# The first FFN of eight items spread anew over ten calls of a macaron block's pipeline

## The chip, the cores and the metric

One core of one Trainium2 chip. The metric is the time of one launch in device microseconds, median of several runs. The engines are named as the profile names them: PE or TensorE (matmuls), DVE or VectorE, ACT or ScalarE, POOL or GpSimd, SP (which here only issues DMAs). Each takes its own instructions in the order in which they are written, and waits on semaphores.

## The reference

Eight items of 256 tokens by 256 features go through one macaron block:

```
x = x + 0.5 * ffn(layernorm(x))     # first FFN
x = x + attn(layernorm(x))          # Mamba mixer and MLP, each with its own rmsnorm and residual
x = x + 0.5 * ffn(layernorm(x))     # second FFN, the same weights
```

`ffn` is a mixture of 32 experts of 96 hidden columns, of which each token uses 6 (sigmoid scores, top 6, normalised), and a shared expert of 192. The kernel computes all experts densely and multiplies by the combine weights, which are zero where an expert isn't used: 3264 hidden columns in 26 chunks of 128. `attn` is a Mamba mixer (512 channels, 16 states, a convolution of 4 taps, a scan over the 256 tokens) and a gated MLP of 1024. Everything is float32, at float32 accuracy.

## The kernel before

**A pipeline over steps.** The outer loop runs over t = -1 to 9. In step t an item t - 1 is in its Mamba mixer, item t - 2 in its MLP, and there is one call of the FFN, whose columns are tokens. A call is narrow (256 columns, one item) or wide (512 columns, two items): `spans` holds the columns of each step. A wide call joins a slot "f1" (columns 0 to 255) and a slot "f2" (columns 256 to 511); both use each chunk's weights once, at half the weight loads per item. Before the change the calls are: step 0 item 0's first FFN, narrow; step 1 items 1 and 2 together, wide; step 2 item 3, narrow; steps 3 to 6 the first FFN of item t + 1 and the second FFN of item t - 3, wide; step 7 the second FFN of items 4 and 5, wide; steps 8 and 9 the second FFN of item 6, then 7, narrow.

**A chunk of a call.** `glu_half` (L737 to L739) makes 6 matmuls for g and 6 for u, float32 split into two parts of fp32r (`x_hi`, `x_lo` times the halves of `wr`). ScalarE takes a tanh (L980) and copies u (L970), VectorE multiplies (L1107), GpSimd multiplies by u (L1376) and by the combine weights (L1384), and four more matmuls (L818) add the down product into `acc`, three chunks later. At the call's end VectorE adds `acc` to the residual (`end`, L1133). Every third chunk has a selection matmul, `cmb`, for the combine weights.

**Step 0** also prepares the weights: each raw chunk is loaded (`raw`, 256 KB), split by ScalarE (`ws`, L949) and VectorE (L1113) into two halves, and the halves are stored to DRAM (`keep_w`, 512 KB), from where all later calls load them (`wl`, `wln`) into six slots. Step 0 has no Mamba and no MLP.

**Norms and routing.** `norm(...)` is four items: mean by a matmul (`n1`), subtraction (`nc`, L1165), variance by a matmul (`n2`), multiply (`nm`, L1176). `routing` is a matmul and eight short pieces on VectorE (`rt1`, `rq`); `rt2` transposes the result into `comb`, `hx` splits the normed x into `x_hi` and `x_lo`. `ln1` and `ln1b` prepare a first FFN, `ln2` and `ln2a` a second.

**Mamba.** `front(0, ...)` and `front(1, ...)` are the projections, convolution and softplus of each half of the channels. Then there are 32 units: in each, two selections by matmul, a multiply, a scan (L1271) and a multiply on VectorE, and a sum on GpSimd. The first front half of an item is either made in the step before ("next", beside the units of the previous item) or, where x1, the result of the first FFN, isn't there in time, in the item's own step before its first unit ("own"). Before the change steps 1 and 2 have an own front half; steps 2 to 7 have a next one.

**The order** of all engines comes from one list per step, `items_of(t)`. `merge(heavy, light, WEIGHT)` lays the light items (Mamba, norms, routing) evenly beside the heavy ones (MLP and FFN) by hand-set lengths; the last `TAIL` = 6 items of the FFN come after all light ones. An own front is at the head of the light list.

**x1 and its residuals.** The first FFN adds into `x1` or into `x1_next`, which is loaded with the item's x beforehand (`again`, `again_n`); `shift` copies `x1_next` to `x1` by a DMA once `r0` has read the old one. `x2kept` holds the residual of the second FFN in slot "f2" (`keep` copies it, `store` writes the output).

Of the kernel before, what the change touches and what calls it, by code (L numbers as in the profile page):

```python
# [33 lines left out]
P = 128  # L34
SEQ, BATCH, DM = 256, 8, 256
# [32 lines left out]
    "again_n": {"x_again_n": 16},  # L68
    "shift": {"shifted": 16},
# [51 lines left out]
STARTS = {"x2_free": 16}  # L121
# [30 lines left out]
def routing(call):  # L152
    return [("rt1", call)] + [("rq", call, i) for i in range(len(ROUTE))]
# [59 lines left out]

def items_of(t):


    if t < 0:
        return [("load", 0)] + norm("ln1") + routing("f1")
# [104 lines left out]
def ffn_items(t):  # L323
# [6 lines left out]
    for p in range(FFN_CHUNKS + DLAG):  # L330
        now, before = p < FFN_CHUNKS, 1 <= p <= FFN_CHUNKS
        out += [("cmb", "ff", p // 3)] if p < ROUTED and p % 3 == 0 else []
# [102 lines left out]
def macaron_kernel(nc, d):  # L435
# [8 lines left out]
    spans = [(0, 2 * SEQ if t == 1 or 3 <= t < BATCH else SEQ) for t in times]  # L444
# [3 lines left out]
    with ctx:  # L448
# [29 lines left out]
        x1_next = sb("x1_next", [P, KC, SEQ])  # L478
# [38 lines left out]
        parts = sb("parts", [P, PARTS, 2, SEQ], BF16)  # L517
        rows = nc.dram_tensor("rows", [3, P, PARTS, 2, SEQ], BF16, kind="Internal").ap()
# [105 lines left out]
        def _(sp):  # L624
# [6 lines left out]
            def do(s, it):  # L631
                if it[0] == "load":
# [5 lines left out]
                    item = s.t() + (1 if times[s.n] < 0 or it == ("load", 0) and times[s.n] == 0 else 2)  # L638
                    sp.dma_start(xin[:], d["x"][item]).then_inc(sem["x_loaded"], 16)
                    if s.n == 0:  # L640
# [63 lines left out]
                if it[0] == "shift":  # L704
# [15 lines left out]
            sp.wait_ge(sem["x2_free"], STARTS["x2_free"] + 16 * BATCH)  # L720
# [3 lines left out]
        def _(pe):  # L724
# [18 lines left out]
            def do(s, it):  # L743
# [77 lines left out]
                elif kind_of(it) == "n1c":  # L821
# [4 lines left out]
                    elif it[1] == "lnA":  # L826
                        pe.wait_ge(sem["shifted"], s.count("shifted", ("shift",), 16))
# [18 lines left out]
                elif kind == "rt1":  # L846
                    if s.n == 0:
                        pe.wait_ge(w_small, 16 * 4)
                    norm = next(n for n in NORMS_OF[it[1]] if ("nm", n) in s.at)
                    pe.wait_ge(sem["normed"], s.count("normed", ("nm", norm), 1))  # L850
# [9 lines left out]
                elif kind == "rt2":  # L860
# [6 lines left out]
                    for tt in range(TT):  # L867
# [615 lines left out]
```

## Time and profile before

| | |
|---|---|
| time, median of 3 runs | 1793.62 us (1792.89 to 1794.39) |
| the profiled execution | 1797.3 us, span 1795.5 us |
| mean granted TensorE clock | 0.947 of full speed |
| busy PE, PE weight loads | 1556.8 us (87%), 1136.3 us (63%) |
| busy DVE, ACT, POOL | 1288.6 us (72%), 842.9 us (47%), 993.8 us (55%) |
| moved by DMA | 200.25 MB, mean 112 GB/s |

Busy shares are means over the whole span. A step is taken here as the stretch from one call's last residual addition to the next call's: the ends are at 116.2, 314.8, 528.4, 727.6, 927.3, 1125.6, 1324.6, 1537.6, 1693.8 and 1795.5 us, steps 0 (with -1) to 9. Within a step, "scan 0", "scan 16" and "scan 31" are the starts of the first, the 17th and the last scan of its 32 units. Matmuls are pipelined, so their bars overlap and a busy TensorE need not be at its peak.

### The profile page before, as it was taken

To read this page: it belongs to the slowest core of one execution; us is meant where nothing else is said; L and a number is where in the kernel's file an instruction comes from. 1 tells how busy PE (TensorE), PEld (TensorE's weight loads), DVE (VectorE), ACT (ScalarE), POOL (GpSimd) and SP (SyncE) were. 2 spreads that over 40 slices of the span, in tenths; PEclk is the share of its full clock that TensorE was granted. 3 is DMA by queue.
4 is the path that set the end of the run, shared out by engine and by line. 5 is a ranking of instruction groups with operands and counts; after the bars stand their busy time and mean duration, and the time that the engine had idled before them with its cause. 6 is when DMAs were issued, how large, how long until landed. Compare 5 with 4: busy or idle time off the path is not lost. (4 is left out here: it accounts for less than half of the span.)

```text
span 1795.5 us, 22504 instructions
## 1 busy us (share of the span) xinstructions
PE 1556.8 (87%) x7088; PEld 1136.3 (63%) x7088; DVE 1288.6 (72%) x2085; ACT 842.9 (47%) x1676; POOL 993.8 (55%) x1048
## 2 busy tenths in 40 slices
PE   6878888777788999899998999899985999868979
PEld 5756555655676666666666666666663666647868
DVE  4536995478968878687959887887857776679421
ACT  4434543545624563356534663456433553445323
POOL 2523676345545766376646666476633766348525
PEclk9989999978989999999999999999996999979989
DMA  6863223332332323242333223232321332224434
GB/s 220 318 206 98 78 82 101 96 100 85 101 105 90 115 84 110 70 138 78 111 102 118 83 90 112 85 129 84 105 79 41 123 100 102 82 86 158 145 104 147
DMA packets 72278, 200.25 MB, mean 112 GB/s; under 512 B 9921, under 2 KB 22433, under 8 KB 71777
## 3 DMA queue, kind: packets, MB, share of 16 engines
q1 hardware_dynamic: 63968, 173.65, 29.1%
q0 software_dynamic: 8192, 25.17, 4.8%
q8 instruction: 57, 0.93, 0.2%
q14 instruction: 61, 0.49, 0.1%
HBM read 173.62 MB, written 23.59 MB: 110 GB/s over the span
## 5 line engine op out<-in xcount | busy, mean ns | idle before, releaser
L737 PE MATMUL gub<-x_hi,wr 128*128 128x512 f32 (+1 forms) x1040 | 425.4, 409 | 50.6 <-DVE hid L1107 44.8
L1397 POOL TENSOR_TENSOR ring<-ring 128x512 f32<-128x512 f32 x192 | 253.6, 1321 | 307.4 <-DVE ring L1277 306.2
L1376 POOL TENSOR_TENSOR hid<-hid,u_sb 128x512 f32<-128x512 f32 (+1 forms) x260 | 289.6, 1114 | 236.1 <-ACT u_sb L970 199.0
L818 PE MATMUL acc<-hid,w_down 128*128 128x512 f32 (+1 forms) x1040 | 408.9, 519 | 1.8 <-POOL hid L1376 1.8
L739 PE MATMUL gub<-x_hi,wr 128*128 128x512 f32 (+1 forms) x1040 | 370.8, 357 | 0.0
L738 PE MATMUL gub<-x_lo,wr 128*128 128x512 f32 (+1 forms) x1040 | 370.2, 356 | 0.0
L1271 DVE TENSOR_TENSOR_SCAN ring<-decays,side 128x512 f32<-128x512 f32 x256 | 310.5, 1213 | 28.9 <-ACT decays L1069 24.6
L970 ACT ACTIVATE u_sb<-gub 128x512 f32<-128x512 f32 (+1 forms) x260 | 132.7, 510 | 347.3 <-PE gub L739 346.8
L980 ACT ACTIVATE hid<-gub 128x256 f32<-128x256 f32 (+1 forms) x324 | 156.8, 484 | 278.2 <-PE gub L739 153.7
L1384 POOL TENSOR_TENSOR hid<-hid,weight 128x512 f32<-128x512 f32 (+1 forms) x240 | 272.9, 1137 | 15.8
L737 PEld LDWEIGHTS gub<-x_hi,wr 128*128 128x128 f32 x1040 | 205.4, 197 | 93.6 <-issue 58.1
L818 PEld LDWEIGHTS acc<-hid,w_down 128*128 128x128 f32 x1040 | 189.2, 197 | 97.2 <-issue 80.8
L1069 ACT ACTIVATE decays<-dts,a_neg 128x255 f32<-128x255 f32 x512 | 228.8, 497 | 3.8 <-DVE ring L1271 3.6
L1262 DVE TENSOR_TENSOR side<-dtx,side 128x512 f32<-128x512 f32 x256 | 176.8, 690 | 69.0 <-PE side L912 68.3
L739 PEld LDWEIGHTS gub<-x_hi,wr 128*128 128x128 f32 x1040 | 204.6, 197 | 27.1
L738 PEld LDWEIGHTS gub<-x_lo,wr 128*128 128x128 f32 x1040 | 205.8, 198 | 24.4 <-issue 5.5
L1107 DVE SCALAR_TENSOR_TENSOR hid<-hid,gub 128x512 f32<-128x512 f32 (+1 forms) x260 | 149.0, 573 | 98.3 <-ACT hid L980 98.3
L1277 DVE TENSOR_TENSOR ring<-ring,side 128x512 f32<-128x512 f32 x256 | 176.0, 687 | 59.5 <-PE side L915 36.2
L885 PE MATMUL side<-rn,w_in 128*128 128x256 f32 x448 | 120.4, 417 | 18.7 <-DVE ring L1271 13.5
L912 PE MATMUL side<-bst,sel_b 96*128 96x256 bf16 x512 | 103.7, 285 | 33.9 <-DVE ring L1271 18.1
L915 PE MATMUL side<-cst,sel_c 96*128 96x256 bf16 x512 | 103.9, 286 | 33.2 <-DVE ring L1271 32.7
L779 PE MATMUL gub<-xn_mlp,wm_gu 128*128 128x256 f32 x512 | 122.4, 387 | 0.0
(120 smaller groups left out, 1823.3 us busy)
## 6 DMA issues: line engine op xcount, KB each, us to landing
wr<-w_halves SPq DMA_DIRECT2D x234, 512.0 KB, 3.3
wm_gu<-in_w_mlp POOLq DMA_DIRECT2D x64, 256.0 KB, 3.1
w_halves<-wr SPq DMA_DIRECT2D x26, 512.0 KB, 4.9
wm_down<-in_w_mlp POOLq DMA_DIRECT2D x64, 128.0 KB, 2.6
w_raw<-in_w_gu SPq DMA_DIRECT2D x26, 256.0 KB, 4.3
rows<-parts SPq DMA_DIRECT2D x16, 384.0 KB, 2.3
cst<-rows SPq DMA_DIRECT2D x48, 128.0 KB, 2.6
xin<-in_x SPq DMA_DIRECT2D x8, 256.0 KB, 2.9
```

The costliest lines, as they stand in the source:

```text
L737: mm(out, w[:, 0, half, k, :], x_hi[:, k, a:b], start=(k == 0), stop=False)
L738: mm(out, w[:, 0, half, k, :], x_lo[:, k, a:b], start=False, stop=False)
L739: last = mm(out, w[:, 1, half, k, :], x_hi[:, k, a:b], start=False, stop=(k == KC - 1))
L818: last = mm(acc[k][:, a:b], w, h[:, a:b], start=(c == 0), stop=(c == (MLP_CHUNKS if mlp else FFN_CHUNKS) - 1))
L980: A(hid[c % HSLOTS][:, a:b], s.gub_of(it)[:, a:b], ACT.Tanh, scale=0.5).then_inc(sem["tanh_done"], 1)
L1069: A(decay[u % 2][:, h, 1:SEQ], dts[:, j, 1:SEQ], ACT.Exp, scale=a_neg[:, j, n:n + 1]).then_inc(sem["decay"], 1)
L1262: v.tensor_tensor(b, twice(dtx[:, j, :]), b, ALU.mult).then_inc(sem["driven"], 1)
L1271: v.tensor_tensor_scan(w.rearrange("p h s -> p (h s)"), decay[u % 2][:, :, :].rearrange("p h s -> p (h s)"), s.side_of(("ub", u))[:, :], 0 ...
L1277: v.tensor_tensor(w, w, pair(s.side_of(it)), ALU.mult).then_inc(sem["read_out"], 1)
L1376: nc.gpsimd.tensor_tensor(h, h, u_sb[c % USLOTS][:, a:b], ALU.mult).then_inc(sem["hidden"], 1)
L1384: nc.gpsimd.tensor_tensor(h, h, weight[c // 3 % CSLOTS][:, a:b], ALU.mult).then_inc(sem["weighted"], 1)
L1397: add(ysum, ysum, ring[:, u % 3], ALU.add).then_inc(sem["y_sum"], 1)
```

## The change

The first FFN runs earlier: items 0 and 1, 2 and 3, 4 and 5 as pairs in wide calls of steps 0, 1 and 2, item 6 in step 3 and item 7 in step 4, each beside a second FFN (item t - 3). Steps 5 and 6 have only the second FFN of items 2 and 3, narrow, in columns 256 to 511. Steps 7, 8 and 9 are as before. So there are again ten calls, wide in steps 0, 1, 2, 3, 4 and 7 and narrow in 5, 6, 8 and 9.

With it: both items' norms come before step 0, and their routing is made within step 0, beside chunks 0 to 2, whose `cmb` moves behind them. Step 1 makes a next front half besides its own one, and step 2 no longer has an own one. `ln1` falls from the list of steps 4 and 5; steps -1, 0 and 1 have two. The results of the first FFN wait in DRAM (`x1_kept`): `store_a` and `store_b` write them, `fetch` loads `x1` from there in place of `shift`. `x1_stage` and `x2kept` are the two accumulators of a pair.

```diff
+FIRST = {0: (0, 1), 1: (2, 3), 2: (4, 5), 3: (6,), 4: (7,)}
+NORMED_IN = {-1: (0, 1), 0: (2, 3), 1: (4, 5), 2: (6,), 3: (7,)}
+
+OWN_SLOT = {BATCH - 1: "f1", BATCH: "f1", BATCH + 1: "f1"}
+
+
+def span_of(t):
+    return (SEQ, 2 * SEQ) if t in (5, 6) else (0, SEQ) if t >= BATCH else (0, 2 * SEQ)
+
+
+def place(t, slot):
+
+    return slice(SEQ, 2 * SEQ) if slot == "f2" else slice(0, SEQ), slice(0, SEQ)
+
+
...
-        return [("load", 0)] + norm("ln1") + routing("f1")
+        ln1 = norm("ln1")
+        return [("load", 0)] + ln1[:2] + [("load", 1)] + ln1[2:] + norm("ln1b")
     mamba, mlp = 0 <= t - 1 < BATCH, 0 <= t - 2 < BATCH
 
 
-
-
-
-    first, twin, second, own = t < BATCH - 1, t == 1, 3 <= t < BATCH, t >= BATCH - 1
-    late_front, next_front = 1 <= t <= 2, 2 <= t < BATCH
-    ready = (["f1"] if first else []) + (["f2"] if twin or second else [])
-    hand = [("hx", call) for call in ready] + [("rt2", call) for call in ready]
-    following = t == 0 or t + 2 < BATCH
-    keep = [("keep",)] if second else []
-    keep += [("load", 0)] if following else []
+    own = OWN_SLOT.get(t)
+    next_front = 1 <= t < BATCH
+    ready = (["f1"] if t < 5 else []) + (["f2"] if t < BATCH else [])
+    hand = [("hx", call) for call in ready]
+    hand += [("rt2", call) for call in ready] if t else []
+    keep = [("keep",)] if 3 <= t < BATCH else []
+    fetches = ([("again",), ("again_b",)] if t == 0 else [("again_a",), ("again_b",)] if t < 3 else
+               [("again_a",)] if t in (3, 4) else [])
     turn = [("r0",), ("carry",)] if mamba else []
-    turn += [("again",)] if t < 2 else [("shift",)] if t < BATCH else []
-    turn += [("again_n",)] if 1 <= t < BATCH - 1 else []
+    turn += [("fetch",)] if next_front else []
     ln2 = norm("ln2") + routing("f2") if mlp and not own else []
-    ln1 = norm("ln1") + routing("f1") if following else []
-    if t == 0:
-        ln1 = ln1[:2] + [("load", 1)] + ln1[2:] + norm("ln1b") + routing("f2")
+    ln1 = norm("ln1") + routing("f1") if t in NORMED_IN else []
+    ln1 = [("load", 0)] + ln1 if ln1 else []
+    if t in NORMED_IN and len(NORMED_IN[t]) > 1:
+        ln1 = ln1[:3] + [("load", 1)] + ln1[3:] + norm("ln1b") + routing("f2")
     ahead = [(k, c) for c in range(MSLOTS) for k in ("mgn", "mdn")] if 0 <= t + 1 - 2 < BATCH else []
     ff = ffn_items(t)
-    if not mamba:
-        if t == 0:
-            return hand + keep + merge(ff[:-TAIL], turn + ln1, WEIGHT) + ahead + ff[-TAIL:]
-        return mlp_items() + ahead + norm("ln2a") + routing("f1") + [("rt2", "f1"), ("hx", "f1")] + ff
+    if t == 0:
+        early = [it for call in ("f1", "f2") for it in routing(call, ("early",)) + [("rt2", call)]]
+        at = ff.index(("cmb", "ff", 0))
+        return near(fetches + hand + merge(ff[:at], early, WEIGHT) +
+                    merge(ff[at:-TAIL], ln1, WEIGHT) + ahead + ff[-TAIL:])
+    chain = []
+    if own:
+        chain = (norm("ln2a") + routing("f1") if own == "f1" else norm("ln2") + routing("f2")) + [
+            ("rt2", own), ("hx", own)]
+        chain = mlp_items() + ahead + chain
+        if not mamba:
+            return chain + ff
     follow = norm("lnA") + norm("rms1") + merge(front(0, "next"), ln2, SPACE) if next_front else ln2
-    light = norm("lnO") + norm("rmsO") + front(0, "own") if late_front else []
-    begin = len(light)
+    light = norm("lnO") + norm("rmsO") + front(0, "own") if t == 1 else []
     light += merge(unit_items(0), front(1, "own") + ln1, SPACE)
     light += merge(unit_items(1), follow, SPACE) if follow else unit_items(1)
     light += [("yz", JC - 1), ("outp",)] + norm("rms2")
-    turns = [("end", "mlp")] if mlp else []
-    turns += [("nm", "lnO")] if late_front else []
+    turns = [("end", "mlp")] if mlp else [("nm", "lnO")]
     if not mlp:
-        out = hand + keep + merge(ff[:-TAIL], light, WEIGHT) + ahead + ff[-TAIL:]
+        out = fetches + hand + merge(ff[:-TAIL], light, WEIGHT) + ahead + ff[-TAIL:]
     elif own:
-        chain = mlp_items() + ahead + norm("ln2a") + routing("f1") + [("rt2", "f1"), ("hx", "f1")]
-        cut = begin + len(unit_items(0) + front(1, "own")) * 2 // 3
+        cut = len(unit_items(0) + front(1, "own")) * 2 // 3
         out = hand + keep + merge(chain, light[:cut], WEIGHT) + merge(ff[:-TAIL], light[cut:], WEIGHT) + ff[-TAIL:]
     else:
         heavy = mlp_items() + ahead + ff
-        out = hand + heavy[:6] + keep + merge(heavy[6:-TAIL], light, WEIGHT) + heavy[-TAIL:]
+        out = hand + heavy[:6] + keep + fetches + merge(heavy[6:-TAIL], light, WEIGHT) + heavy[-TAIL:]
     out = near(after(out, turn, *turns))
     if next_front:
 
         at = out.index
-        assert at(("shift",)) < at(("n1", "lnA")) and at(("ub", UNITS // 2)) < at(("split", 0, "next"))
+        assert at(("fetch",)) < at(("n1", "lnA")) and at(("ub", UNITS // 2)) < at(("split", 0, "next"))
         assert at(("yz", 1)) < min(at(("xc", 0, "next", 0)), at(("z", 0, "next")))
     if ln2:
         assert out.index(("end", "mlp")) < out.index(("n1", "ln2"))
...
+        late = splits and p < 3
+        out += [("cmb", "ff", p // 3)] if p < ROUTED and p % 3 == 0 and not late else []
         out += [("g", "ff", p)] if now else []
         out += [("by_u", "ff", p - 1)] if before else []
-        out += [("by_comb", "ff", p - 1)] if 1 <= p <= ROUTED else []
+        out += [("by_comb", "ff", p - 1)] if 1 <= p <= ROUTED and not late else []
         out += [("down", "ff", p - DLAG)] if p >= DLAG else []
         out += [("by_g", "ff", p), ("u", "ff", p)] if now else []
+        if late and p == 2:
+            out += [("cmb", "ff", 0), ("by_comb", "ff", 0), ("by_comb", "ff", 1)]
         if splits:
             out += [("keep_w", p)] if now else []
             out += [("raw", p + RAWS)] if p + RAWS < FFN_CHUNKS else []
@@ -343,15 +371,17 @@
             out += [("wl", p + WSLOTS)]
         if now and more and p == last_in(p % WSLOTS):
             out += [("wln", p % WSLOTS)]
-    if t < BATCH - 1:
-        out += [("end", "f1" if t < 2 else "f1n")]
-    if t == 1:
-        out += [("end", "f1b")]
+    if t < 5:
+        out += [("end", "f1" if t == 0 else "f1n")]
+    if t in (1, 2, 3, 4):
+        out += [("store_a",)]
+    if t < 3:
+        out += [("end", "f1b"), ("store_b",)]
     if 3 <= t < BATCH:
         out += [("end", "f2"), ("store",)]
-    return out + ([("end", "f2a"), ("store_own",)] if t >= BATCH - 1 else [])
-
-
+    if t in OWN_SLOT:
+        out += [("end", "f2a")]
+    return out + ([("store_own",)] if t in OWN_SLOT else [])
...
-    spans = [(0, 2 * SEQ if t == 1 or 3 <= t < BATCH else SEQ) for t in times]
+    spans = [span_of(t) for t in times]
     led = Ledger(steps, TURNS, LOOP)
 
     ctx = ExitStack()
...
+                if it[0] == "fetch":
+
 
                     sp.wait_ge(sem["r_base"], s.count("r_base", ("r0",), 1))
-                    sp.dma_start(x1[:], x1_next[:]).then_inc(sem["shifted"], 16)
-                if it[0] == "again_n":
-                    if ("shift",) in s.at:
-                        sp.wait_ge(sem["shifted"], s.count("shifted", ("shift",), 16))
-                    sp.dma_start(x1_next[:], d["x"][s.t() + 1]).then_inc(sem["x_again_n"], 16)
+                    stored = "b_stored" if s.t() in (1, 3, 5) else "a_stored"
+                    sp.wait_ge(sem[stored], s.prior(stored))
+                    sp.dma_start(x1[:], x1_kept[s.t()]).then_inc(sem["fetched"], 16)
+                if it[0] == "again_a":
+                    if (least := s.prior("a_stored")) is not None:
+                        sp.wait_ge(sem["a_stored"], least)
+                    sp.dma_start(x1_stage[:], d["x"][FIRST[s.t()][0]]).then_inc(sem["x_again_a"], 16)
+                if it[0] == "again_b":
+                    if (least := s.prior("b_stored")) is not None:
+                        sp.wait_ge(sem["b_stored"], least)
+                    sp.dma_start(x2kept[:], d["x"][FIRST[s.t()][1]]).then_inc(sem["x_again_b"], 16)
+                if it[0] == "store_a":
+                    sp.wait_ge(sem["residual"], s.count("residual", ("end", "f1n"), KC))
+                    sp.dma_start(x1_kept[FIRST[s.t()][0]], x1_stage[:]).then_inc(sem["a_stored"], 16)
+                if it[0] == "store_b":
+                    sp.wait_ge(sem["residual"], s.count("residual", ("end", "f1b"), KC))
+                    sp.dma_start(x1_kept[FIRST[s.t()][1]], x2kept[:]).then_inc(sem["b_stored"], 16)
```

## Rows read from the trace of the kernel before

**Rows 1.** The stretches view, one window for each step; columns stand in its first line.
```profile
core 0: us, PE busy (x) PEld busy (x) DVE busy (x) ACT busy (x) POOL busy (x), PEclk, DMA share, GB/s
0.00:116.20 116.20, 84.89 (x478) 75.68 (x478) 50.20 (x137) 47.82 (x106) 42.96 (x54) 0.93 0.75 259
116.20:314.80 198.60, 171.52 (x673) 111.64 (x674) 144.35 (x210) 93.81 (x177) 113.00 (x98) 0.95 0.30 98
314.80:528.40 213.60, 160.46 (x825) 132.19 (x825) 162.81 (x270) 104.72 (x218) 95.49 (x118) 0.87 0.31 98
528.40:727.60 199.20, 185.36 (x785) 126.98 (x784) 159.86 (x252) 101.28 (x191) 121.90 (x118) 0.99 0.30 97
...
927.30:1125.60 198.30, 185.99 (x782) 127.44 (x781) 158.62 (x251) 101.37 (x191) 121.69 (x118) 0.98 0.31 101
1125.60:1324.60 199.00, 182.39 (x764) 123.97 (x763) 155.72 (x229) 97.79 (x185) 122.10 (x118) 0.99 0.31 99
```

**Rows 2.** The same view, step 6 cut at scans 0, 16 and 31.
```profile
1125.60:1135.40 9.80, 8.79 (x43) 7.33 (x41) 6.50 (x17) 3.72 (x9) 3.89 (x10) 1.00 0.44 130
1135.40:1206.50 71.10, 64.09 (x282) 44.46 (x283) 64.12 (x90) 33.82 (x69) 47.09 (x53) 0.98 0.34 110
1206.50:1296.40 89.90, 83.08 (x345) 54.56 (x345) 71.14 (x103) 52.12 (x96) 59.90 (x47) 1.00 0.29 95
1296.40:1324.60 28.20, 26.42 (x98) 17.62 (x96) 13.95 (x22) 8.13 (x12) 11.21 (x10) 1.00 0.22 74
```

**Rows 3.** The same view, step 2 from its first scan on.
```profile
361.50:436.80 75.30, 55.42 (x294) 44.34 (x293) 66.20 (x104) 34.73 (x79) 37.66 (x39) 0.82 0.31 100
436.80:507.60 70.80, 53.79 (x297) 44.65 (x298) 63.70 (x101) 41.67 (x88) 36.31 (x38) 0.88 0.29 94
507.60:528.40 20.80, 15.96 (x81) 13.57 (x80) 10.78 (x20) 5.68 (x10) 6.62 (x8) 0.92 0.31 105
```

**Rows 4.** The same view, step 1 cut at scans 0, 16 and 31.
```profile
116.20:165.00 48.80, 39.79 (x145) 28.74 (x146) 24.02 (x41) 27.31 (x46) 16.42 (x12) 0.91 0.42 137
165.00:243.50 78.50, 68.28 (x284) 43.33 (x283) 69.57 (x101) 39.80 (x78) 46.05 (x37) 0.97 0.24 79
243.50:288.80 45.30, 40.85 (x170) 24.42 (x171) 42.51 (x56) 19.85 (x43) 35.60 (x29) 0.96 0.24 80
288.80:314.80 26.00, 22.61 (x77) 15.15 (x76) 8.25 (x15) 6.86 (x10) 14.92 (x22) 0.93 0.36 116
```

**Rows 5.** Groups by form: VectorE busy us, mean ns, then idle before and its releaser.
```profile
L1107 DVE SCALAR_TENSOR_TENSOR hid<-hid,gub 128x512 f32<-128x512 f32 x156 | 105.9, 679 | 32.9 <-ACT hid L980 32.9
...
L1107 DVE SCALAR_TENSOR_TENSOR hid<-hid,gub 128x256 f32<-128x256 f32 x104 | 43.1, 415 | 65.3 <-ACT hid L980 65.3
```

**Rows 6.** Timeline of TensorE, wide FFN in step 3: start, length, instruction.
```profile
600.86 0.48 PE L737 MATMUL gub<-x_hi,wr 128*128 128x512 f32 x1
...
603.91 1.88 PE L818 MATMUL acc<-hid,w_down 128*128 128x512 f32 x4
605.63 0.39 PE L915 MATMUL side<-cst,sel_c 96*128 96x256 bf16 x2
```

**Rows 7.** Timeline of several engines, step 0: start, length, instruction, idle before.
```profile
6.39 0.69 DVE L1165 TENSOR_TENSOR xc_f<-xin,side 128x512 f32<-128x512 f32 x1 [0.69 <-PE side L835]
12.21 0.69 DVE L1176 TENSOR_TENSOR xc_f<-xc_f,rstd 128x512 f32<-128x512 f32 x1 [5.13 <-ACT rstd L998]
...
19.09 0.23 DVE L1341 TENSOR_TENSOR c_f<-cm,c_f 128x64 bf16<-128x64 f32 x1
...
22.32 0.78 PE L737 MATMUL gub<-x_hi,wr 128*128 128x256 f32 x1
...
94.62 0.63 ACT L949 ACTIVATE wr<-w_raw 128x512 fp32r<-128x512 f32 x1 [5.12 <-DMA w_raw<-in_w_gu]
...
115.47 0.76 DVE L1133 SCALAR_TENSOR_TENSOR x<-acc,x 128x256 f32<-128x256 f32 x2 [3.92 <-PE acc L818]
```

**Rows 8.** DMA issues: tensor, queue, count, size, us from issue to landing.
```profile
x<-x_next SPq DMA_DIRECT2D x6, 256.0 KB, 3.8
```

More of the change, by code:

```diff
@@ L67 @@
     "again": {"x_again": 16},
-    "again_n": {"x_again_n": 16},
-    "shift": {"shifted": 16},
+    "again_a": {"x_again_a": 16},
+    "again_b": {"x_again_b": 16},
+    "store_a": {"a_stored": 16},
+    "store_b": {"b_stored": 16},
+    "fetch": {"fetched": 16},
     "hx": {"x_hi": 1, "x_split": 1},
@@ L119 @@
 }
-STARTS = {"x2_free": 16}
+STARTS = {}
 def kind_of(item):
@@ L149, in norm, with routing @@
     return [("n1", which)] + centred + [("n2", which), ("nm", which)]
-def routing(call):
-    return [("rt1", call)] + [("rq", call, i) for i in range(len(ROUTE))]
+def routing(call, when=()):
+    return [("rt1", call) + when] + [("rq", call, i) + when for i in range(len(ROUTE))]
 def unit_items(half):
@@ L477, in macaron_kernel @@
         x1 = sb("x1", [P, KC, SEQ])
-        x1_next = sb("x1_next", [P, KC, SEQ])
+        x1_stage = sb("x1_stage", [P, KC, SEQ])
         hn = sb("hn", [P, KC, SEQ])
@@ L517, in macaron_kernel @@
         parts = sb("parts", [P, PARTS, 2, SEQ], BF16)
+        x1_kept = nc.dram_tensor("x1_kept", [BATCH, P, KC, SEQ], F32, kind="Internal").ap()
         rows = nc.dram_tensor("rows", [3, P, PARTS, 2, SEQ], BF16, kind="Internal").ap()
@@ L637, in do @@
                         sp.wait_ge(sem["centered"], least)
-                    item = s.t() + (1 if times[s.n] < 0 or it == ("load", 0) and times[s.n] == 0 else 2)
-                    sp.dma_start(xin[:], d["x"][item]).then_inc(sem["x_loaded"], 16)
-                    if s.n == 0:
+                    sp.dma_start(xin[:], d["x"][NORMED_IN[s.t()][it[1]]]).then_inc(sem["x_loaded"], 16)
+                    if s.n == 0 and it[1] == 0:
                         for name, t in (("w_router", w_router), ("vecs", vecs), ("lnw", lnw),
@@ L719, in _ @@
             walk(sp, do)
-            sp.wait_ge(sem["x2_free"], STARTS["x2_free"] + 16 * BATCH)
+            sp.wait_ge(sem["x2_free"], 16 * BATCH)
         @block.tensor
@@ L826, in do @@
                     elif it[1] == "lnA":
-                        pe.wait_ge(sem["shifted"], s.count("shifted", ("shift",), 16))
+                        pe.wait_ge(sem["fetched"], s.count("fetched", ("fetch",), 16))
                     elif it[1] == "lnO":
@@ L846, in do @@
                 elif kind == "rt1":
-                    if s.n == 0:
+                    if s.n == 1:
                         pe.wait_ge(w_small, 16 * 4)
-                    norm = next(n for n in NORMS_OF[it[1]] if ("nm", n) in s.at)
-                    pe.wait_ge(sem["normed"], s.count("normed", ("nm", norm), 1))
+                    pe.wait_ge(sem["normed"], s.count("normed", it, 0))
                     for over, least in s.last_use("side", it):
@@ L866, in do @@
                     b = s.side_of(it)[:, :].bitcast(BF16)
-                    for tt in range(TT):
-                        last = nc.tensor.transpose(b[0:PARTS * EXPERTS, tt * P:(tt + 1) * P],
-                                                   c3[it[1]][:, tt, :], ident[:])
+                    tokens = place(s.t(), it[1])[1]
+                    for at in range(tokens.start, tokens.stop, P):
+                        to = at - tokens.start
+                        last = nc.tensor.transpose(b[0:PARTS * EXPERTS, to:to + P], c3[it[1]][:, at // P, :], ident[:])
                     last.then_inc(sem["side_filled"], 1)
@@ L1119, in do @@
                     dve.wait_ge(sem["down_done"], s.count("down_done", last, 1))
-                    a = SEQ if call in ("f1b", "f2") else 0
                     src, dst, scale = {"f1": (x1, x1, 0.25), "mlp": (res, x2, 0.5),
-                                       "f1b": (x1_next, x1_next, 0.25), "f1n": (x1_next, x1_next, 0.25),
+                                       "f1b": (x2kept, x2kept, 0.25), "f1n": (x1_stage, x1_stage, 0.25),
                                        "f2a": (x2, x2, 0.25), "f2": (x2kept, x2kept, 0.25)}[call]
+                    slot = {"f1": "f1", "f1n": "f1", "f1b": "f2", "f2": "f2",
+                            "f2a": OWN_SLOT.get(s.t())}.get(call)
+                    cols, tokens = (slice(0, SEQ), slice(0, SEQ)) if call == "mlp" else place(s.t(), slot)
                     if call == "mlp" and times[s.n] >= BATCH:
@@ L1130, in do @@
                     if call in ("f1b", "f1n"):
-                        dve.wait_ge(sem["x_again_n"], s.count("x_again_n", ("again_n",), 16))
+                        again = "x_again_b" if call == "f1b" else "x_again_a"
+                        dve.wait_ge(sem[again], s.count(again, it, 0))
                     for k in range(KC):
-                        v.scalar_tensor_tensor(dst[:, k, :], acc[k][:, a:a + SEQ], scale, src[:, k, :],
+                        v.scalar_tensor_tensor(dst[:, k, tokens], acc[k][:, cols], scale, src[:, k, tokens],
                                                ALU.mult, ALU.add).then_inc(sem["residual"], 1)
                 elif kind == "hx":
-                    src, a = xc[it[1]], 0 if it[1] == "f1" else SEQ
+                    cols, tokens = place(s.t(), it[1])
+                    src = xc[it[1]][:, :, tokens]
                     dve.wait_ge(sem["normed"], s.count("normed", it, 0))
-                    v.tensor_copy(x_hi[:, :, a:a + SEQ], src[:]).then_inc(sem["x_hi"], 1)
+                    v.tensor_copy(x_hi[:, :, cols], src).then_inc(sem["x_hi"], 1)
                     dve.wait_ge(sem["x_hi"], s.count("x_hi", it, 1))
-                    v.tensor_tensor(x_lo[:, :, a:a + SEQ], src[:], x_hi[:, :, a:a + SEQ].bitcast(F32),
+                    v.tensor_tensor(x_lo[:, :, cols], src, x_hi[:, :, cols].bitcast(F32),
                                     ALU.subtract).then_inc(sem["x_split"], 1)
                 elif kind == "keep":
-                    dve.wait_ge(sem["x2_free"], s.prior("x2_free"))
+                    stored = "b_stored" if s.t() == 3 else "x2_free"
+                    dve.wait_ge(sem[stored], s.prior(stored))
                     v.tensor_copy(x2kept[:], x2[:]).then_inc(sem["kept"], 1)
@@ L1180, in do @@
                     dve.wait_ge(sem["side_filled"], s.count("side_filled", it, 1))
-                    a = 0 if it[1] == "f1" else SEQ
+                    cols = place(s.t(), it[1])[0]
                     if (least := s.prior("comb_filled")) is not None:
                         dve.wait_ge(sem["comb_filled"], least)
-                    v.tensor_copy(comb[:, a:a + SEQ], s.side_of(it)[:, :].bitcast(BF16)[0:PARTS * EXPERTS, 0:SEQ]
+                    wide = cols.stop - cols.start
+                    v.tensor_copy(comb[:, cols], s.side_of(it)[:, :].bitcast(BF16)[0:PARTS * EXPERTS, 0:wide]
                                   ).then_inc(sem["comb_ready"], 1)
@@ L1306, in route @@
                 if piece == 0:
-                    dve.wait_ge(sem["rt_exp"], s.count("rt_exp", ("rt1", it[1]), 1))
+                    dve.wait_ge(sem["rt_exp"], s.count("rt_exp", ("rt1", it[1]) + it[3:], 1))
                     link(v.tensor_scalar(e_sc[:], e_sc[:], 1.0, None, ALU.add))
```

3 lines of the change are left out of this document (removed).

## The prediction

> **What bounds the kernel now.** I read the stretches view first, one window for each of the ten steps, because a step is the unit that the change moves work between [rows 1]. TensorE's busy time alone (93% in step 3) says little, since a matmul's bar overlaps the next one, so I went to the start times of one wide FFN chunk: 605.63 - 600.86 = 4.77 us, of which about 0.2 is a unit's two selections, leaves 4.55 us of back-to-back issue [rows 6]. 26 chunks make 118 us, and the eight selections of the combine weights (0.25 us) make 120. The MLP adds 96 matmuls of half a wide one's 0.43 us (21 us), Mamba with norms and routing about 40 us by the same prices, so steps 3 to 6 issue about 180 of their 199 us: these are TensorE's. In step 6 after scan 16, VectorE is busy for 71.1 of 89.9 us at a granted clock of 1.00; it is waiting for TensorE there [rows 2].
>
> A narrow step with Mamba in it is another matter. In step 2 between scans 0 and 31, VectorE is busy for 66.2 of 75.3 and 63.7 of 70.8 us, about 0.9, and TensorE has idle time [rows 3]. There VectorE is the limit. And step 0 is neither: ScalarE waits 5.12 us for a raw weight, with the DMA engines busy for a share of 0.75 [rows 1, 7]. So narrow calls save TensorE time that steps 5 and 6 can use only until VectorE becomes the limit, and step 0 has some cover to give.
>
> The ten calls stay ten, six wide and four narrow; TensorE's, ScalarE's and GpSimd's sums hardly change. What changes is the neighbour of each call.
>
> **Step 0 becomes wide.** Before the first chunk there is a second norm. The first takes VectorE from 6.39 to 12.90 us [rows 7]; it can't begin the second before it has done the first's last multiply, so the second ends at about 12.9 + 6.5 = 19.4. Two splits of 1.1 us and the first weight's subtraction of 0.7 follow: first chunk at about 23.1, against 22.32 before. The routing, which held the start until 19.3, now lies beside chunks 0 to 2. TensorE passes through the items in order, so it can stand at the second transpose; chain by chain I get 3 us there and 1 us at the first down product. The chunks issue for 120 us. Two norms (16 matmuls of 0.215 us, half of a wide one's 0.43, [rows 6]) and four routings (32 short ones near 0.1 us) add 7. The start at half clock costs 3, small waits behind ScalarE another 3. Raw loads and stores of halves took 93 us before and lie under that. The last down product ends at 23.1 + 120 + 7 + 3 + 4 + 3 = 160, and both residuals at 161 instead of 116.2: **+44 us** (bounds +38, no stalls, and +52, a stall of the routing's full chain at each transpose). The extra loads of x, 256 KB each on SP's queue ahead of the raw weights, have until 19 us; they cost nothing, or 3 us (an SBUF-sized transfer lands in 3.8 us, [rows 8]) if the first weight is late.
>
> **Step 1** keeps its wide call and its own front half, and gains the next item's front half and a second norm with routing; it still has no MLP. Its first part (48.8 us) is set by the chain of its own front; a slightly smaller share of the FFN falls into it: 47.5 [rows 4]. Scans 0 to 16 run at a VectorE share of 0.89; the added norm and routing is 4 us of VectorE (between 2.9, the difference of steps 5 and 6 [rows 1], and 7, the first one's chain): 82.5. Scans 16 to 31 took 45.3 with nothing beside them; step 2 shows 70.8 with the next front and a norm with routing [rows 3, 4]. Less that norm (4) and with wide multiplies (0.264 us more each [rows 5], two or three chunks fewer), 68. Tail 26. Sum 224: **+25 us**. TensorE gets 56 more matmuls of 0.215 us and eight short ones, 12 us; if that were all, the step would last 211. It isn't the limit: its bars covered 0.86 of step 1 before, and would cover about 0.82 after. Bounds +12 and +33.
>
> **Step 2** loses its own front half and becomes wide. That is the make-up of step 3, 199.2 against 213.6: **-14.4 us** (bounds -17 and -10, for the two stores and loads through DRAM). Here x1 is written at the end of a step and fetched after r0 of a later one. The fetch takes the place of an SBUF copy that landed in 3.8 us [rows 8]. Behind the wait of a store or a load on SP's queue are weight loads of the next call, which run six chunks, over 25 us, ahead. The keep copy of step 3 waits for a store, as it does in every later step. All this I cost at nothing; if the six chunks weren't there it would be one landing, 4 us a step.
>
> **Steps 3 and 4** keep width and neighbours. Step 4 only loses a norm with routing, as step 6 lacks it before: 199.0 against 198.3 in step 5, nothing [rows 1].
>
> **Steps 5 and 6** go narrow. I take step 6's four parts and make VectorE the limit [rows 2]. The multiply falls from 679 to 415 ns [rows 5]: 26 x 0.264 = 6.9 us, of which some 2.4, 3.7 and 0.8 in the last three parts. First part 9.8, minus one split: 9. Scans 0 to 16: 64.1 - 2.4 + 7.5 of waits (7.0 there now, 9.1 in step 2) = 69. Scans 16 to 31: 71.1 - 3.7 + 7.1 (step 2's waits) = 74.5. Tail: 28.2 shrinks to the level of step 2's 20.8, 21.5 [rows 3]. Sum 174 against 198.3 and 199.0: **-50 us** for both. TensorE's saving alone, 57 us a step, would give 142; VectorE's own 147 us forbids it. Bounds: 163 (its waits as few as in scans 16 to 31 of step 1, 2.8 in 45.3 us, [rows 4]) and 190 (VectorE at the 0.76 of all of step 2), which is -71 and -17.
>
> In step 2 the granted clock is 0.87, in step 3 0.99 [rows 1]; between scans 0 and 16 of step 2 it is 0.82, so TensorE is at 1.2 GHz for over a third of it after its waits. The Trainium skill, TensorE: Matmul & The Clock Gate, section "What's actually happening", says that the slow clock is the default and activity releases it. By that rule steps 5 and 6 fall to step 2's clock, and the trace of step 2 agrees. My parts are taken at that clock already, so the sum by the rule and by the rows is the same 174; at the slow bound it is the 190.
>
> Steps 7, 8 and 9 stay. Sum: 44 + 25 - 14 - 50 = **+5 us**. The profiled execution ran 1797.3 us (span 1795.5), the median is 1793.62; the difference goes on the median: **1798.5 us**.
>
> **Rivals.** (a) Faster: VectorE in steps 5 and 6 waits less than in step 2, since no own front stands ahead and more of the FFN lies between the units to fill TensorE's queue. Each at 168 or less turns the sign by itself (two steps, 6 us each: 5 - 12 = -7, 1787). Scans 16 to 31 of step 1 speak for it, both halves of step 2 against. The point from which it decides is 170 us a step. (b) Faster by the port: in the narrow steps GpSimd's multiplies are half as long, and VectorE's xs, dtx and parts operations with two SBUF inputs would be held up less; from busy time per step that is at most 3 us a step, 1792 from my sum. The Trainium skill, SBUF — State Buffer, section "SBUF: two separate sides", has VectorE and GpSimd share a port pair as an exclusive lock; no row here isolates it. (c) Faster: step 1 is held by TensorE alone and grows by 12: 1786. Its VectorE share of 0.89 and 0.94 from scan 0 on speaks against. (d) Slower: in steps 5 and 6 TensorE, in order and often at 1.2 GHz, holds VectorE at 0.76: 1831. (e) Slower: routing and weight preparation stall step 0 by 8 us more: 1806. (f) No change: the terms cancel, within 3.6 us. That the work isn't moved as described I can exclude; the spans of the calls are constants.
>
> **How the numbers follow.** Forecast 0.40, its own range 1790 to 1807; (a) 0.17, (b) 0.07, (c) 0.10, (d) 0.10, (e) 0.16. A measurement of this kernel tells about 0.2% (3.6 us) from no change. Of the forecast's 0.40 about 0.18 lies within that and 0.02 below it, of (b) 0.05 within, of (c) and (a) 0.02. Faster 0.29, same 0.25, slower 0.46. The range 1781 to 1815 reaches over (a), (b), (c) and (e), and leaves out (d) and the far ends of steps 1, 5 and 6.
>
> **What would show it.** Right: step 0 ends near 161 with TensorE's starts 4.6 us apart per chunk; step 1 lasts near 224 with VectorE around 0.73; step 2 near 199; steps 5 and 6 near 174 with VectorE over 0.8 and a clock under 0.93. Wrong: if steps 5 and 6 are at 165 or at 185; if step 1 is at 211; if TensorE in step 0 waits for raw weights. The likeliest error is the two large terms of opposite sign, 44 + 25 and 50, each of which may be off by ten.

## The result, and the profile after

The changed kernel takes 1844.57 us (median of 4 runs, 1835.98 to 1847.22) against 1794.01 us before: a ratio of 1.0273, 95% interval 1.0236 to 1.0310. It is 51 us slower. The forecast was 1798.5 us and a range to 1815.

The stretches view of the changed kernel, one window for each step as in [rows 1]; the columns are the same:

```profile
0.00:161.60 161.60, 141.56 (x496) 95.57 (x496) 76.82 (x164) 67.08 (x112) 70.64 (x54) 0.94 0.58 197
161.60:396.00 234.40, 190.87 (x739) 127.51 (x740) 169.52 (x257) 115.34 (x210) 115.18 (x98) 0.93 0.26 84
396.00:610.70 214.70, 194.35 (x778) 131.76 (x777) 162.51 (x250) 101.31 (x191) 120.98 (x118) 0.94 0.30 98
610.70:818.40 207.70, 188.01 (x782) 128.35 (x781) 160.00 (x252) 101.11 (x191) 121.28 (x118) 0.98 0.30 97
818.40:1021.80 203.40, 184.04 (x764) 125.30 (x763) 159.17 (x229) 97.22 (x185) 121.80 (x118) 0.98 0.30 98
1021.80:1199.00 177.20, 139.59 (x765) 115.95 (x764) 141.90 (x223) 83.21 (x185) 94.50 (x118) 0.90 0.33 110
1199.00:1373.30 174.30, 136.09 (x764) 113.08 (x763) 142.48 (x224) 83.20 (x185) 94.48 (x118) 0.93 0.34 111
```

Taken against [rows 1], and with the forecast of each step beside it:

| step | before | forecast | after | missed by |
|---|---|---|---|---|
| 0 | 116.2 | 161 | 161.6 | 1 |
| 1 | 198.6 | 224 | 234.4 | 10 |
| 2 | 213.6 | 199 | 214.7 | 16 |
| 3 | 199.2 | 199 | 207.7 | 9 |
| 4 | 199.7 | 199 | 203.4 | 4 |
| 5 | 198.3 | 174 | 177.2 | 3 |
| 6 | 199.0 | 174 | 174.3 | 0 |
| 7 to 9 | 470.9 | 471 | 471.9 | 1 |

The two large terms, +44 for step 0 and -50 for steps 5 and 6, came out at +45 and -46. Some 29 us of the miss lie where I had taken a step's length over from another and costed nothing: steps 2, 3 and 4 do the same work as steps 3 to 6 did before, apart from loads, stores and fetches, and take 4 to 16 us longer. Another 10 us are in step 1. Step 3 is the cleanest pair, item for item the same work before and after. These are its parts after, cut at scans 0, 16 and 31 (stretches view):

```profile
610.70:621.40 10.70, 9.63 (x47) 8.06 (x45) 6.66 (x18) 2.92 (x7) 4.12 (x10) 1.00 0.49 150
621.40:705.00 83.60, 73.38 (x316) 51.26 (x316) 70.41 (x114) 40.30 (x80) 51.47 (x57) 0.96 0.30 99
705.00:793.40 88.40, 82.11 (x338) 54.32 (x339) 71.22 (x102) 50.44 (x94) 55.09 (x43) 0.98 0.28 91
793.40:818.40 25.00, 22.89 (x83) 14.71 (x82) 11.71 (x22) 7.45 (x11) 10.61 (x9) 1.00 0.27 91
```

The same two halves, scans 0 to 16 and 16 to 31, in the kernel before:

```profile
538.90:618.70 79.80, 71.47 (x316) 50.29 (x316) 72.59 (x115) 40.47 (x80) 52.14 (x57) 0.98 0.33 105
618.70:700.90 82.20, 78.61 (x330) 51.68 (x330) 67.55 (x102) 49.75 (x93) 54.96 (x43) 1.00 0.30 97
```

VectorE has as much to do as before in the whole step (160.0 against 159.86 us), but idles for 13 and 17 us in the two halves, where it idled for 7 and 15. The waits view of VectorE in step 3, of the changed kernel (us in total, times, longest):

```profile
DVE side L1312 <- PE side L955: 19.4, 12, 3.1
DVE x_stage L1179 <- PE acc L861: 7.8, 1, 7.8
DVE ring L1327 <- PE side L958: 5.5, 7, 1.7
```

and of the kernel before, same step:

```profile
DVE side L1262 <- PE side L912: 8.1, 10, 1.5
DVE ring L1271 <- ACT decays L1069: 5.2, 4, 2.1
DVE ring L1277 <- PE side L915: 4.6, 4, 1.4
DVE x_next L1133 <- PE acc L818: 4.2, 1, 4.2
```

The wait that has grown is that of a unit's first multiply for its selection matmul, from 8.1 to 19.4 us, and in the longest case from 1.5 to 3.1 us, two thirds of a chunk. TensorE has little more to do (busy for 188.0 us, 185.4 before, in a step that is 8.5 us longer); it comes to the selections later. In one of the long waits it goes through a down product and eight matmuls of the next front before it reaches the selection that VectorE waits for (timelines of TensorE and VectorE, changed kernel):

```profile
722.11 1.88 PE L861 MATMUL acc<-hid,w_down 128*128 128x512 f32 x4
723.83 1.89 PE L928 MATMUL side<-rn,w_in 128*128 128x256 f32 x8
725.56 0.39 PE L955 MATMUL side<-bst,sel_b 96*128 96x256 bf16 x2
725.98 0.70 DVE L1312 TENSOR_TENSOR side<-dtx,side 128x512 f32<-128x512 f32 x1 [2.91 <-PE side L955]
```

TensorE's timeline in step 3 shows one more stall, for x:

```profile
668.41 0.39 PE L782 MATMUL gub<-x_hi,wr 128*128 128x512 f32 x1
671.46 1.13 PE L878 MATMUL side<-xin,mean_w 128*128 128x256 f32 x4 [2.66 <-DMA xin<-in_x]
```

and SP's timeline shows why it lands so late:

```profile
663.69 3.84 SPq L702 DMA_DIRECT2D wr<-w_halves  x3
667.57 0.43 SPq L669 DMA_DIRECT2D xin<-in_x  x1
```

The load of `xin` used to be issued at the step's start. In the changed list it stands right ahead of the mean that reads it, and SP issues it behind three weight loads, 1.2 us before TensorE is ready for that mean.

**The theory from there.** `items_of` leaves the last TAIL = 6 items of the FFN behind the light items and spreads the light items over the rest. Before, the six in steps 3 to 6 were three down products, two ends and a store. The change adds `store_a` (and `store_b`) to the list's end, and they count among the six. So only two down products stay in the tail, the stretch over which the light items are spread gets longer by one down product, and every light item comes a fraction of a chunk later against the FFN. Around unit 22 of step 3 TensorE's list changes like this, from the two programs' lists (the light `cmb` item ahead of g 15 is left out):

```
before: g 14 | unit 22 | down 11 | ub 23 | u 14 | g 15 | unit 23 | down 12 | ub 24 | u 15
after:  down 11 | unit 22 | u 14 | ub 23 | g 15 | down 12 | unit 23 | u 15 | ub 24 | g 16
```

Compared over all of step 3, 39 pairs of a selection's item and a matmul item of the MLP or the FFN have changed places, 13 of them with a down product, and in every one the selection now comes behind the matmul that it preceded.

I call this the theory of the order. Its rival is the theory of the DRAM way: loads, stores and fetches of x1 delay SP's queue, or what waits for them.

### The profile page after: what moved, and what is told of

It is laid out like the page before. It is cut to its first block and busy times, and to the rows that moved or that the text cites. A ratio compares the mean times of both kernels' runs of the same rounds, so it can differ in the third digit from the quotient of the medians.

```text
span 1845.2 us, 22514 instructions
## 1 busy us (share of the span) xinstructions
PE 1573.7 (85%) x7088; PEld 1148.0 (62%) x7088; DVE 1311.1 (71%) x2084; ACT 843.0 (46%) x1676; POOL 993.3 (54%) x1048
## 5 line engine op out<-in xcount | busy, mean ns | idle before, releaser
L780 PE MATMUL gub<-x_hi,wr 128*128 128x512 f32 (+1 forms) x1040 | 433.9, 417 | 37.4 <-DVE hid L1149 34.7
L782 PE MATMUL gub<-x_hi,wr 128*128 128x512 f32 (+1 forms) x1040 | 371.5, 357 | 0.0
```

The source lines that it names most:

```text
L780: mm(out, w[:, 0, half, k, :], x_hi[:, k, a:b], start=(k == 0), stop=False)
L782: last = mm(out, w[:, 1, half, k, :], x_hi[:, k, a:b], start=False, stop=(k == KC - 1))
```

## The experiments

**e1_tail, e2_load, e3_both, e4_before_tail5.** One edit each, the third has both, the fourth edits the kernel before. In e1_tail, `tail` is then used in place of `TAIL` in steps 1 to 6 (those lines are left out here):

```diff
 e1_tail
+    tail = TAIL + (1 if t in (1, 2, 3, 4) else 0)
 ...
 e2_load
-    ln1 = [("load", 0)] + ln1 if ln1 else []
+    if ln1:
+        fetches = fetches + [("load", 0)]
     if t in NORMED_IN and len(NORMED_IN[t]) > 1:
-        ln1 = ln1[:3] + [("load", 1)] + ln1[3:] + norm("ln1b") + routing("f2")
+        ln1 = ln1[:2] + [("load", 1)] + ln1[2:] + norm("ln1b") + routing("f2")
 e4_before_tail5
-TAIL = 6
+TAIL = 5
```

> The changed kernel with one down product more behind the light items in steps 1 to 4 (the added stores no longer count among the last six). Its list in step 4 then is that of step 6 of the kernel before, item by item, apart from the loads and stores. Theory of the order (the two stores shift every light item half a chunk later against the FFN, and VectorE's units then wait for TensorE more): step 4 falls from 203.3 to 199, step 3 from 207.8 to about 202, step 2 from 214.7 to about 204, step 1 by a few us; about 1822 us. Theory of the DRAM way (fetches, loads and stores of x1 delay SP's queue): no change, 1845.

> The changed kernel with the load of xin put at the step's start again, instead of right ahead of the mean that reads it, in steps 0 to 3. Theory of the order: only the 2.8 us wait of TensorE for xin goes, once in each of steps 1 to 3 and at most twice in step 0; about 1836 us, the rest of the loss stays. Rival: the late load is the whole loss of steps 2 and 3 through what queues behind it; then step 3 is at 200, step 4 stays at 203, and the time is about 1820.

> Both edits together. Steps 3 and 4 then have the order of steps 3 and 6 of the kernel before in full, with the DRAM way of x1 still in place. Theory of the order: steps 2, 3 and 4 at 199 to 200, the time about 1810 us; what is left over the kernel before is in steps 0 and 1. Theory of the DRAM way: steps 2 to 4 stay 4 to 15 us longer than those, 1840 or more.

> The kernel before with TAIL = 5 instead of 6, nothing else. Theory of the order: steps 3 to 6 of it get 4 to 5 us longer each, the others less; about 1815 us. Theory of the DRAM way, or any other that lies in the moved work: no change, 1794.

| kernel | median us | ratio to before, interval | steps 1, 2, 3, 4 |
|---|---|---|---|
| after | 1844.57 | 1.0273 (1.0236 to 1.0310) | 234.4, 214.7, 207.7, 203.4 |
| e1_tail | 1818.81 | 1.0131 (1.0108 to 1.0154) | 227.4, 204.9, 203.5, 200.5 |
| e2_load | 1828.66 | 1.0182 (1.0156 to 1.0208) | 229.7, 208.6, 204.7, 202.4 |
| e3_both | 1812.21 | 1.0089 (1.0060 to 1.0118) | 231.4, 202.5, 197.4, 199.0 |
| e4_before_tail5 | 1827.87 | 1.0179 (1.0156 to 1.0202) | 197.3, 215.5, 202.4, 208.9 |

The order it is. With both edits, the lists of steps 3 and 4 are those of steps 3 and 6 of the kernel before, item for item, apart from the loads, stores and fetches. These steps then last what the same work lasted before, 199.2 and 199.0 us, with the DRAM way in place:

```profile
593.40:790.80 197.40, 185.90 (x781) 127.05 (x780) 158.80 (x251) 101.19 (x191) 121.77 (x118) 0.98 0.31 102
790.80:989.80 199.00, 182.37 (x764) 123.95 (x763) 155.66 (x229) 97.66 (x185) 122.08 (x118) 0.99 0.30 100
```

and the selection wait of step 3 (waits view, e3_both) is back at its old size:

```profile
DVE side L1314 <- PE side L957: 9.2, 11, 1.5
```

The fourth run is the strongest: one number in the kernel before, no work moved, costs 32 us. I had expected 21; its steps 4 and 5 grow by 9 and 10 us each, where I had put 4 to 5. Its waits in step 4 have the same signature as the changed kernel's:

```profile
DVE side L1262 <- PE side L912: 16.6, 12, 2.9
DVE x_next L1133 <- PE acc L818: 7.8, 1, 7.8
```

e2_load gave back 16 us by the difference of medians, where I had expected 9; its rival, all of the loss in steps 2 and 3, would have given back 25. TensorE's waits for `xin` in steps 1, 2 and 3 of the changed kernel are 4.1, 2.6 and 2.7 us, and these steps get 4.7, 6.1 and 3.0 us shorter. The two edits give 26 and 16 us alone and 32 together, so what they mend overlaps.

**e10_before_load.** The same place of the load, tried in the kernel before:

```diff
-    keep += [("load", 0)] if following else []
+    keep += [("load", 0)] if t == 0 else []
 ...
+    ln1 = [("load", 0)] + ln1 if ln1 and t else ln1
```

> The kernel before with the load of xin in steps 1 to 5 moved from the start of the step to right ahead of the mean that reads it, nothing else. If the place of the load alone costs what e2_load gave back, 2.8 us of TensorE's wait in each of five steps and a little order: plus 12 to 20 us, 1806 to 1814. If e2_load gained through something in the moved work: 1794.

1817.32 us, ratio 1.0115 (1.0098 to 1.0132), 3 us above the range that I had put. Steps 1 to 5 take 202.1, 214.8, 206.3, 205.1 and 203.6 us, and the 16 units of the first half of step 3 took 88.3 us against 79.8. So the load's place costs 4 to 7 us a step in steps 1 and 3 to 5; the narrow step 2 pays 1. TensorE's stalls for `xin` in these five steps are 1.6, 3.1, 6.1, 4.8 and 2.7 us, 18 in all, of the 22.5 that the steps lose. The trace shows one part of what comes on top: for about 5 us behind the stalls of steps 3 and 5 the granted clock is 0.54 and 0.50 of full speed, so TensorE goes on at 1.2 GHz (stretches view of this run, first behind the stall of step 3, then behind that of step 5):

```profile
595.20:600.00 4.80, 4.80 (x10) 2.78 (x11) 2.28 (x4) 0.63 (x1) 0.00 (x0) 0.54 0.00 0
600.00:605.00 5.00, 5.00 (x25) 3.58 (x24) 3.87 (x6) 2.70 (x5) 2.65 (x2) 1.00 0.31 107
1003.10:1008.00 4.90, 4.88 (x10) 2.70 (x11) 2.34 (x4) 0.63 (x1) 2.00 (x2) 0.50 0.01 2
```

In the changed kernel the clock is 0.50 for 5.1 us behind the stall of step 1 and 0.72 for 5.4 us behind that of step 2; behind that of step 3 it stays at 1.00, and there e2_load gained little more than the stall.

**e9_before_tail7, e11_tail8.** One item to the other side: TAIL = 7 in the kernel before, and (on top of e8_tail56 below) `TAIL + 2` in steps 1 to 4 of the changed one.

> The kernel before with TAIL = 7, the light items a little earlier against the FFN instead of later. The list around units 22 to 24 of step 3 is nearly that of TAIL = 6 (one item moves past its neighbour now and then), while TAIL = 5 exchanged the order of selections and down products. If the loss comes from that exchange, TAIL 7 is within 5 us of the kernel before: 1789 to 1799. If any other place than 6 is worse, as far as 5 was (32 us): 1815 or more.

> e8_tail56 with one more down product behind the light items of steps 1 to 4 (4 in all). By the theory of the order, with the list nearly the same as at 3 in steps 2 to 4: within 5 us of e8_tail56, 1802 to 1812. It is also the last try at a version of the changed kernel near the kernel before; it can't pass it unless steps 0 and 1 shrink by 15 us, which nothing in it does.

e9 takes 1790.80 us, a ratio of 0.9976 (0.9963 to 0.9988), and e11 1804.73 us, 1.0049 (1.0033 to 1.0064). Both as expected. In steps 3 to 6 of e9 the order of selections and matmuls is nearly that of the kernel before (1 pair exchanged in steps 3 to 5, 5 pairs in step 6), and these steps are within 1.5 us of their length there. In its steps 2 and 7 the order does change: 34 and 21 pairs are exchanged, with the selection now ahead of the matmul, and the steps take 212.4 and 211.0 us against 213.6 and 213.0. So not every exchange costs time: the ones that cost it in these runs put the selection behind. e9 is the only kernel here that beats the kernel before, by 0.24%, which is about what the medians of the kernel before differ from one measurement to another (1792.27 to 1795.99); it has nothing of the change. Most of the difference between the two profiled executions is in step 0, 108.8 us at a granted clock of 0.97 against 116.2 at 0.93, although that step's list is the same but for one pair of items.

**e5_fetch_x.** The DRAM way, by itself, on e3_both. The fetch takes x from the input, without waiting for a store, so this kernel leaves the first FFN out of what items 1 to 7 bring into the mixer. The work is the same otherwise:

```diff
-                    stored = "b_stored" if s.t() in (1, 3, 5) else "a_stored"
-                    sp.wait_ge(sem[stored], s.prior(stored))
-                    sp.dma_start(x1[:], x1_kept[s.t()]).then_inc(sem["fetched"], 16)
+                    sp.dma_start(x1[:], d["x"][s.t()]).then_inc(sem["fetched"], 16)
```

> e3_both with the fetch of x1 taken from the input x, without waiting for the stores of x1 (so that items 1 to 7 go into the mixer without their first FFN; the stores still run). Everything else, order too, is as in e3_both. Theory of the order: no change, 1812 us within 3. Theory of the DRAM way: the wait for a store on SP's queue goes, and the time falls by up to 4 us a step, to 1790 to 1800.

1810.55 us beside 1812.21 of e3_both (ratios 1.0105 and 1.0089, whose intervals overlap widely). Steps 2 to 4 take 200.5, 199.7 and 199.0, 599.2 in all against 598.9 in e3_both. The fetch's wait for a store costs nothing that can be measured. The stores, the extra loads and a fetch from DRAM were left in, so that part is judged only by steps 3 and 4 of e3_both.

**e7_ln1b_late.** With the order mended, step 1 is the last that misses its forecast. On e3_both, its second norm with routing moves from the first 16 units to the second 16:

```diff
-        ln1 = ln1[:2] + [("load", 1)] + ln1[2:] + norm("ln1b") + routing("f2")
+        ln1 = ln1[:2] + [("load", 1)] + ln1[2:]
+        if t == 1:
+            ln2 = norm("ln1b") + routing("f2")
+        else:
+            ln1 += norm("ln1b") + routing("f2")
 ...
```

> e3_both with the second norm and its routing (ln1b) of step 1 moved from the first 16 units to the second 16. The first half holds the own second front half and ln1; scans 0 to 16 took 89.3 us in e3_both against 78.5 before, where the sum gave 4 us for this norm. If it costs 11 us there because it crowds the shared banks of the small matmuls, the first half falls to about 79 and the second rises by 5 to 8: step 1 at 224 to 228, total about 1807. If it is VectorE's work alone, 4 us move from one half to the other: no change.

1812.03 us: no change, but both halves speak. These are its stretches in step 1, up to scan 31 and cut at scans 0 and 16; the same in e3_both stand below them:

```profile
161.40:209.60 48.20, 35.52 (x134) 26.36 (x135) 23.29 (x39) 25.61 (x43) 14.62 (x10) 0.92 0.34 117
209.60:288.40 78.80, 66.25 (x264) 42.40 (x263) 70.71 (x102) 37.87 (x74) 45.08 (x36) 0.92 0.23 74
288.40:366.30 77.90, 66.03 (x272) 43.45 (x273) 69.64 (x98) 45.41 (x85) 43.60 (x34) 0.96 0.23 75
```

```profile
159.50:210.70 51.20, 38.32 (x134) 28.32 (x135) 23.28 (x40) 25.71 (x43) 14.63 (x10) 0.87 0.31 101
210.70:300.00 89.30, 76.40 (x297) 49.28 (x296) 76.35 (x126) 43.69 (x83) 47.81 (x38) 0.90 0.21 71
300.00:366.90 66.90, 55.90 (x242) 36.65 (x242) 61.44 (x79) 39.78 (x76) 41.30 (x32) 1.00 0.25 81
```

The first half falls from 89.3 to 78.8, its length in [rows 4], and the second rises from 66.9 to 77.9. A norm with its routing costs 11 us in either place, not 4: in the second half VectorE is busy for 8.2 us more and idle for 2.8 us more, and in the first it is busy for 5.6 us less and idle for 4.9 us less. Neither of my two readings had this, and the guess that the norm crowds one half falls.

**e6_own2.** Item 1's first front half goes back from step 1 ("next") to step 2 ("own"), on e3_both:

```diff
-    next_front = 1 <= t < BATCH
+    late_front, next_front = 1 <= t <= 2, 2 <= t < BATCH
 ...
```

> e3_both with the next front half of item 1 taken out of step 1 and made in step 2 as an own one, as in the kernel before. If the next front half in step 1 costs what the sum said (20 us) and step 2 without an own front half is worth 14, the total gets 0 to 5 us shorter: step 1 at 209 to 213, step 2 at 218 to 224. Rival: in wide step 2, which is TensorE's, the own front half costs much more than it did in the narrow one, since the MLP and the wide FFN wait in TensorE's list behind its chain: step 2 at 235 or more, the total at 1825.

1829.79 us, ratio 1.0212 (1.0191 to 1.0232): the rival holds. The two steps:

```profile
161.30:373.00 211.70, 176.37 (x686) 115.11 (x687) 151.83 (x232) 98.46 (x183) 112.13 (x97) 0.94 0.26 86
373.00:613.70 240.70, 206.04 (x835) 142.37 (x834) 178.04 (x276) 118.56 (x218) 124.19 (x120) 0.94 0.29 93
```

Without the next front half step 1 is 20 us shorter; scans 16 to 31 alone fall by 21.7 us, from 66.9 to 45.2, where the sum had 22.7 (68 against 45.3). In wide step 2 an own one costs 38 us (240.7 against 202.5), where I had expected 16 to 22.

**e8_tail56.** The order in the narrow steps: `TAIL - 1` in steps 5 and 6, on e3_both. The last six items there were `by_u`, three down products, an end and a store, so the edit takes only `by_u` out of them.

> e3_both with the last-items count at 5 in steps 5 and 6, so that three down products, end and store lie behind the light items there as in the wide steps of the kernel before. Theory of the order: VectorE's waits in the second half (11 to 13 us in the changed kernel, where 7 were expected) fall, the second half goes from 77 to about 73; total about 1806. If the narrow steps have enough TensorE time to spare, the order matters little there: 1812.

1806.96 us, ratio 1.0085 (1.0066 to 1.0104). Beside e5 and e7 (1810.55 and 1812.03) it is 4 to 5 us faster, but steps 5 and 6 account for only 2 to 3 of that (173.0 and 172.1 against 173.6 and 174.2 of e7), and their second half stays at 76.2. The theory's 1806 was hit by luck: it gave a second half of 73. The rest is in steps 0 and 1, which vary by 3 us from run to run. Inconclusive, and a weak test: the edit exchanges only 5 pairs of a selection and a matmul in each of these steps, so what it costs to put many selections behind in a narrow step was not tried.

## Why the prediction was wrong

By its own steps:

**Step 0, +44: right.** Measured +45.4. The second norm ended at 18.8 us instead of 19.4, and the first chunk began at 22.44 instead of 23.1; the terms that I gave for it, 19.4, twice 1.1 and 0.7, add up to 22.3 (timelines of VectorE and TensorE, changed kernel):

```profile
18.11 0.69 DVE L1225 TENSOR_TENSOR xc_f<-xc_f,rstd 128x512 f32<-128x512 f32 x1 [4.53 <-ACT rstd L1041]
```

```profile
22.44 0.77 PE L780 MATMUL gub<-x_hi,wr 128*128 128x512 f32 x1 [1.65 <-DVE wr L1155]
```

ScalarE's waits for raw weights fell from 19.5 us in all (22 to 116 us of the kernel before) to 2.8 (23 to 160 us), so the DMA cover went to TensorE as forecast; with the wide call TensorE is busy for 141.6 of the 161.6 us.

**Steps 5 and 6, -50: right.** Measured -45.8. The two halves of step 6 took 64.1 and 76.2 us where the sum had 69 and 74.5, and the tail 23.6 for 21.5. The granted clock fell as weighed, to 0.90 and 0.93 from 0.98 and 0.99, though not down to step 2's 0.87, which the sum had taken.

**Steps 3 and 4, "keep width and neighbours": the step that failed.** The prediction costed them at nothing because it took the make-up of a step for its length. Length depends on the order of the list and on the place of a load too, and the added stores had shifted the list: that cost 8.5 us in step 3 and, with no such load, 3.7 in step 4. e3_both restores both and gets 197.4 and 199.0.

**Step 2, -14.4: failed for the same reason.** Measured +1.1. With both edits it takes 202.5 us in e3_both, and 200.5, 201.7, 200.6 and 199.6 in e5, e7, e8 and e11, so -11 to -14, inside my range for it. Both edits together are worth 32 us of the 51 (1844.57 to 1812.21).

**The DRAM way at nothing: right**, as far as e5_fetch_x and steps 3 and 4 of e3_both show.

**Step 1, +25: mechanism right, one term mis-sized.** The stretch with the next front half was put at 68 us and took 66.0, and the half front is worth 20 us of the step (e6_own2). The norm with routing was priced at 4 and costs 11 (e7_ln1b_late): VectorE's busy time for it, 5.6 to 8.2 us, was put too low, and the 3 to 5 us that the units wait with it were left out. The rest of the +35.8, about 5 us, goes with the order and the stall for `xin`, as far as one can tell: the step is 227.4 to 231.4 in e1 to e3, 3 to 7 us shorter, but it also varies by 3 us between kernels that share its list.

**The rivals.** None of them was it. (d) had a time near the measured one (1831) and the same wait, VectorE for TensorE, but put it in steps 5 and 6 through the clock; it came in steps 1 to 4 through the list. A sum of 1812, what e3_both takes, would have been within the range: 16 us over before for the change proper, where the forecast said 5.

**What stays open.** Which of the exchanged pairs in the list costs how much. e1 to e4, e9 and e11 tell the order apart from everything else, but no run exchanges one pair alone. The same 39 exchanges cost 3 us in step 3 of e4_before_tail5 and 9 and 10 us in its steps 4 and 5, and no run shows why. Nor did any run take the two parts of the price of a late load, the stall and the slower clock behind it, one by one. And e3_both is still 16 us over the kernel before: steps 0 and 1 cost 43 and 33 us there, steps 2, 5 and 6 give back 11, 22 and 25.

## What to carry to other kernels

In a kernel whose engines take their instructions from one list written out in advance, a bookkeeping item counts: a store appended to the end slid the interleaved work by a fraction of a chunk, and putting that right alone (e1_tail) gave back 26 of the 51 us. Before pricing a step as "the same work as that one", compare the two lists item by item, not only their sums, and try the constants of the interleaving again after each change. A load goes into the list where its transfer is hidden, not where its data is needed; on a shared queue it starts behind whatever stands ahead of it. Here that alone was worth 16 us (e2_load).

## What the runs showed of the hardware

TensorE's clock followed the stalls that the order made. In step 2 the granted clock was 0.94 in the changed kernel and 0.97 in e3_both, with the same matmuls, and e10_before_load shows the 1.2 GHz level, at 0.54 and 0.50, for about 5 us right behind two of its stalls. So part of a lost microsecond is paid again. The four runs of the changed kernel spread over 11 us (0.6%), those of the kernel before over 3 us beside them but over up to 8 us beside the later kernels, so that the change makes the time less steady is not shown.
